# One DMA moved ahead of four others, and the softmax sums of an attention block joined in another order

## The chip, the cores and the metric

The kernel runs on one core of one Trainium2 chip. The metric is the device time of one execution in microseconds (us), as the median of several runs; lower is better.

## The reference

The program computes two transformer layers on one sequence of 2048 tokens with 128 features. The change concerns the first part, the attention of layer 0, and the code just behind it. Cut to what matters:

```python
q = concat([q_c, q_r]);  k = concat([k_c, k_r])        # 8 heads, 128 + 32 features
scores = einsum('bhsd,bhtd->bhst', q, k) * scale       # 2048 x 2048 for each head
attn = softmax(scores, axis=-1)
o = einsum('bhst,bhtd->bhsd', attn, v_c)
x = x + o.reshape(b, s, N_HEADS * D_K) @ W_O + b_O     # then FFN, anchor attention, FFN
```

## The kernel before, in words

The attention works in `NBLK` = 32 blocks: 8 heads times 4 groups of 512 queries. In a block n, the scores stand transposed: 16 tiles of 128 keys by 512 queries. TensorE (PE) makes each with `scores(n, t)` (L1385), ScalarE (ACT) takes the exponential into the ring `prob` (L577), and PE multiplies by the values in two halves of 8 tiles, `weighted(n, 0)` and `weighted(n, 1)` (L1429).

The maximum over the keys must be known before the exponential. So PE also makes the scores in the other orientation (`half_rows`, L1371), and VectorE (DVE) reduces each half row to its maximum (`chunk_max`, L971). These run `LEAD` = 10 slots ahead of the block that uses them. When the maxima of block n+1 are complete, DVE writes `nmx` (`minus_max`, L979), and the sync engine (SP) issues one DMA that copies the 512 values into one row of `q_cols`, the shift row (L463). The first `scores` of block n+1 waits for that DMA. An 8-slot loop on PE and on DVE (`for slot in range(CPB)`) fixes which work stands where: a slot has two score tiles and two half rows. The multiplications by the values stand in slots 1 and 6; `output` (L1413) in slot 3, `totals` (L1440) in slot 4. DVE does `minus_max` in slot 5.

The denominators are the sums of `prob` over the keys. The 16 tiles are first added in 4 groups of 4 tiles (`part`), then `totals` sums each over its partitions. GpSimd (POOL) does these additions in `sums` (L853, L858); for the groups in `VSUM` DVE does the first of three (`begin_sum`, L986), in slots 5 and 6. ACT copies the totals to `den_sb` (L563), SP issues four DMAs (L451, `denominators`) that spread them over partitions, DVE inverts them (L1004, L1006) and adds the scaled output to `X` (`accumulate`, L1020).

SP does its DMAs strictly in program order. In iteration n its loop has the four DMAs of `denominators(n - 2)` first and the shift row of block n after them. In the last block, n = 31, the sums don't go through POOL at all: PE multiplies the 16 `prob` tiles by ones (`last_totals`, L1450), four at a time. Between the blocks PE also takes the transposes of the next layernorm (`ln0_pe`, L337).

PE's results lie in eight banks of PSUM. Half rows, keys, outputs and totals take turns in four of them, so each waits until the item four before it in the turn has been read (`bank_read`).

Of the kernel before, what the change touches and what calls it, by code (L numbers as in the profile page):

```python
# [5 lines left out]
ALU = mybir.AluOpType  # L6
# [6 lines left out]
P = 128  # L13
# [5 lines left out]
def build_kernel(nc, d, out):  # L19
# [13 lines left out]
    with ctx:  # L33
# [157 lines left out]
        VSUM = (2, 3)  # L191
# [7 lines left out]
        part = sb("part", [P, 2, NG, BLK])  # L199
        den_sb = sb("den_sb", [P, BLK])  # L200
# [199 lines left out]
        with nc.Block() as block:  # L400
            @block.sync
            def _(sp):
# [50 lines left out]
                for n in range(NBLK):  # L453
                    k = n % NB
                    if n >= 2:
                        denominators(n - 2)
                    sp.wait_ge(s_sel, n + 1)
                    if n < NB:
                        sp.wait_ge(s_qcol, k + 1)
                    else:  # L460
                        sp.wait_ge(s_sc, NT * (n - NB + 1))
                    with nc.allow_non_contiguous_dma("128 x 4 words into one row"):
                        sp.dma_start(q_cols[SH:SH + 1, k, :].bitcast(F32).rearrange("a (p i) -> a p i", i=TPB),  # L463
                                     nmx[:, n % 2, :].bitcast(F32)).then_inc(s_shift, 16)

# [17 lines left out]
            def _(act):  # L483
# [84 lines left out]
                def exponential(n, t):  # L568
                    g = NT * n + t
                    act.wait_ge(s_sc, g + 1)  # L570
                    if g >= RING and t == 0:
                        act.wait_ge(s_pv, NW * (n - 1) + 1)
                        act.wait_ge(s_sum, ADDS * (n - 1) + 6)
# [30 lines left out]
                for n in range(NBLK):  # L604
                    for t in range(NT):
# [11 lines left out]
                        if n == NBLK - 1 and t == 8:  # L617
                            ln0_act(act, 0, 3)
# [138 lines left out]
            def _(pool):  # L757
# [84 lines left out]
                def sums(n, g):  # L842

                    total = part[:, n % 2, g, :]
                    p = [prob[:, (NT * n + t) % RING, :] for t in range(NG * g, NG * (g + 1))]
                    done = ADDS * n + 3 * g - sum(x < g for x in VSUM)
                    if n >= 2 and g == 0:
                        pool.wait_ge(s_ones, n - 1)
                    if g in VSUM:
                        pool.wait_ge(s_sumd, len(VSUM) * n + VSUM.index(g) + 1)  # L850
                    else:
                        pool.wait_ge(s_exp, NT * n + NG * g + 2)
                        pool.tensor_tensor(total, p[0], p[1], ALU.add).then_inc(s_sum, 1)  # L853
                        done += 1
                        pool.wait_ge(s_sum, done)
                    for x in (2, 3):
                        pool.wait_ge(s_exp, NT * n + NG * g + x + 1)
                        pool.tensor_tensor(total, total, p[x], ALU.add).then_inc(s_sum, 1)  # L858
                        done += 1
                        pool.wait_ge(s_sum, done)  # L860

                for n in range(NBLK - 1):
                    for g in range(NG):
                        sums(n, g)
                        if g == 0 and n < 2:
                            columns(n + 2)
                        if n == NBLK - 2 and g >= 2:
                            ln0_pool(pool, g - 2)
# [52 lines left out]
            def _(dve):  # L921
# [141 lines left out]
                for n in range(NBLK):  # L1063
                    for slot in range(CPB):
# [239 lines left out]
            def _(pe):  # L1304
# [138 lines left out]
                def last_totals(g):  # L1443

                    n = NBLK - 1
                    if g == 0:
                        bank_read(("sums", n))
                    pe.wait_ge(s_exp, NT * n + NG * (g + 1))
                    for x in range(NG):
                        last = pe.matmul(ps[C * x:C * (x + 1), BANK["sums", n], :], ones_v[:, :], prob[:, (NT * n + NG * g + x) % RING, :],  # L1450
                                         start=(g == 0), stop=(g == NG - 1))
                    if g == NG - 1:
                        last.then_inc(s_ones, 1)

# [81 lines left out]
                for n in range(NBLK):  # L1536
                    for slot in range(CPB):
# [33 lines left out]
                        if n == NBLK - 1:  # L1571
                            if slot == 2:
                                last_totals(0)
                                bank_read(("norm", 0))
                                ln0_pe(pe, 0, 3)
                            elif slot == 3:
                                totals(n - 1)
                            elif slot == 4:
                                last_totals(1)
                            elif slot == 7:  # L1580
# [4 lines left out]
                                weigh(n, range(2 * NG, 3 * NG))  # L1585
                last_totals(3)
# [5 lines left out]
                pe.wait_ge(ld_l0, 16 * N_LD_L0)  # L1592
                pe.transpose(ps[0:A, 0, 0:A], anchor[:, :], ident[0:A, 0:A])
                pe.transpose(ps[:, 0, AT_GATE:AT_GATE + E], gate0[:, :], ident[0:E, 0:E]).then_inc(s_an_ps, 1)
                last_denominators()
                output(NBLK - 1)
# [331 lines left out]
```

## Time and profile before

| what | value |
|---|---|
| median of 3 runs | 770.61 us (770.42 to 771.03) |
| the profiled execution's own time | 775.4 us |
| its span in the trace | 773.7 us |
| PE busy (matmuls) | 737.8 us, 95% |
| DVE busy | 626.3 us, 81% |
| POOL busy | 577.4 us, 75% |
| ACT busy | 473.2 us, 61% |
| blocks 2 to 31 of the attention | about 67 to 516 us of the span |

PE's matmuls are pipelined, and the busy time counts overlapping ones, so 95% does not say that PE never waits. A row of a timeline gives the start, the duration, the engine and line, and in brackets how long the engine had been idle before and what ended that. Times of a DMA row on SPq are those of its issue; the landing is told apart.

### The profile page before, as it was taken

How to read it: one execution, taken by the hardware profiler on the slowest of the kernel's cores; microseconds unless marked ns; L12 is line 12 of the kernel's file. 1: busy time of each engine (PE TensorE's matmuls, PEld its weight loads, DVE VectorE, ACT ScalarE, POOL GpSimd, SP SyncE). 2: the span in 40 equal slices, each digit the busy share in tenths (PEclk: the TensorE clock that was granted, in tenths of full speed). 3: DMA queues.
4: the chain of work that ended last, by engine and by line, in shares of the span. 5: the costliest groups of instructions: out<-in, count | busy, mean ns of one | idle time of the engine just before them, and what ended most of it. 6: DMA issues, size and time to landing. Idle time of an engine off the chain costs nothing.

```text
span 773.7 us, 12688 instructions
## 1 busy us (share of the span) xinstructions
PE 737.8 (95%) x4214; PEld 468.8 (61%) x4214; DVE 626.3 (81%) x1305; ACT 473.2 (61%) x1067; POOL 577.4 (75%) x478
## 2 busy tenths in 40 slices
PE   7999999999999999999999999999799999999997
PEld 6655555545545555555554555456556689778885
DVE  7889899998999898999999999933887736876564
ACT  4377666767767666776776766663677841454443
POOL 6489889988989989898998898911689861445554
PEclk9999999999999999999999999997999999999999
DMA  7200000000000000000000000003000000000000
GB/s 155 73 2 1 2 2 2 2 3 1 1 3 1 1 2 2 1 2 2 2 2 3 1 1 2 1 22 93 1 1 0 2 1 2 0 1 16 0 14 27
DMA packets 36616, 8.71 MB, mean 11 GB/s; under 512 B 26580, under 2 KB 35813, under 8 KB 36552
## 3 DMA queue, kind: packets, MB, share of 16 engines
q1 hardware_dynamic: 35272, 7.80, 5.0%
q8 instruction: 33, 0.54, 0.3%
q10 hardware_dynamic: 1280, 0.12, 0.1%
q14 instruction: 31, 0.25, 0.1%
HBM read 6.53 MB, written 1.05 MB: 10 GB/s over the span
## 4 chain that ended last, share of the span: by engine, by line
PE 51%; POOL 12%; issue 10%; DMA 9%; SPq 9%; DVE 5%; ACT 3%; POOLq 0%; DVEq 0%
PE ps L1385 11%; PE ps L1371 10%; SPq L451 9%; DMA q_cols<-nmx 8%; PE ps L1429 8%; POOL hid_lo L917 7%; PE ps L1440 4%; PE ps L1775 4%; PE ps L1413 4%; ACT den_sb L563 2%; POOL nrm L899 2%; POOL hid L899 1%; PE ps L1358 1%; PE ps L1359 1%; DVE mx L971 1%
## 5 line engine op out<-in xcount | busy, mean ns | idle before, releaser
L858 POOL TENSOR_TENSOR part<-part,prob 128x512 f32<-128x512 f32 x248 | 329.3, 1328 | 44.7 <-DVE part L986 17.2
L971 DVE TENSOR_REDUCE mx<-ps 128x1 f32<-128x512 f32 x492 | 310.4, 681 | 36.3 <-PE ps L1371 32.5
L577 ACT ACTIVATE prob<-ps 128x512 f32<-128x512 f32 x512 | 271.1, 604 | 95.6 <-PE ps L1385 95.6
L1385 PE MATMUL ps<-q_cols,key 128*128 128x512 f32 x512 | 217.1, 427 | 13.1 <-DMA q_cols<-nmx 10.8
L1371 PE MATMUL ps<-key,q_rows 128*128 128x512 f32 x512 | 201.3, 397 | 0.8 <-DVE key L957 0.4
L1385 PEld LDWEIGHTS ps<-q_cols,key 128*128 128x128 f32 x512 | 95.5, 188 | 123.0 <-issue 49.9
L1429 PE MATMUL ps<-prob,val 128*32 128x512 f32 x1024 | 123.3, 598 | 0.0
L1371 PEld LDWEIGHTS ps<-key,q_rows 128*128 128x128 f32 x512 | 95.9, 188 | 19.2 <-DVE mx L965 1.4
L917 POOL TENSOR_TENSOR hid_lo<-hid,hid_hi 128x512 fp32r<-128x512 f32 x44 | 56.8, 1295 | 49.6 <-ACT hid_hi L734 49.6
L853 POOL TENSOR_TENSOR part<-prob 128x512 f32<-128x512 f32 x62 | 79.7, 1285 | 4.8
L1429 PEld LDWEIGHTS ps<-prob,val 128*32 128x32 f32 x1024 | 26.7, 109 | 60.9 <-issue 59.6
L718 ACT ACTIVATE act_g<-ps 128x512 f32<-128x512 f32 x44 | 26.4, 599 | 50.8 <-PE ps L1815 50.8
L986 DVE TENSOR_TENSOR part<-prob 128x512 f32<-128x512 f32 x62 | 55.6, 898 | 0.3 <-ACT prob L577 0.3
L1275 DVE TENSOR_TENSOR prod<-ps,act_g 128x512 f32<-128x512 f32 x44 | 30.3, 690 | 31.2 <-PE ps L1815 27.5
L691 ACT ACTIVATE pT<-ps 128x128 f32<-128x128 f32 x128 | 33.7, 279 | 10.6 <-PE ps L1752 10.6
L555 ACT COPY u_sb<-ps 128x512 f32<-128x512 f32 x32 | 18.8, 588 | 34.1 <-PE ps L1429 34.1
L1020 DVE SCALAR_TENSOR_TENSOR X<-ps,rden,X 128x128 f32<-128x128 f32 x128 | 35.7, 341 | 1.3 <-PE ps L1413 1.2
L1813 PE MATMUL ps<-hT_hi,w_hi 128*128 128x512 f32 x88 | 35.4, 403 | 0.0
L1413 PEld LDWEIGHTS ps<-proj,u_sb 128*128 128x128 f32 x256 | 33.4, 191 | 2.6
L1814 PE MATMUL ps<-hT_hi,w_lo 128*128 128x512 f32 x88 | 34.7, 394 | 0.0
L1815 PE MATMUL ps<-hT_lo,w_hi 128*128 128x512 f32 x88 | 34.6, 394 | 0.0
L1413 PE MATMUL ps<-proj,u_sb 128*128 128x128 f32 x256 | 33.8, 275 | 0.0
(278 smaller groups left out, 1085.8 us busy)
## 6 DMA issues: line engine op xcount, KB each, us to landing
den<-den_sb SPq DMA_DIRECT2D x124, 2.0 KB, 2.1
X<-in_L_attn_h_t_dram SPq DMA_DIRECT2D x4, 256.0 KB, 4.4
out_dram<-X SPq DMA_DIRECT2D x4, 256.0 KB, 2.3
w_raw<-in_L_ffn_w_g_dram SPq DMA_DIRECT2D x1, 704.0 KB, 4.4
w_raw<-in_L_ffn_w_u_dram SPq DMA_DIRECT2D x1, 704.0 KB, 7.6
w_raw<-in_L_ffn_w_d_dram SPq DMA_DIRECT2D x1, 704.0 KB, 9.0
w_o<-in_L_attn_W_O_dram SPq DMA_DIRECT2D x1, 512.0 KB
w_out<-in_L_attn_W_out_dram SPq DMA_DIRECT2D x1, 512.0 KB, 5.0
```

What stands on the lines that cost most here:

```text
L451: sp.dma_start(den[:, n % 2, g, :], den_sb[C * g:C * g + 1, :].rearrange("a (p i) -> a p i", i=TPB)).then_inc(s_dend, 16)
L577: act.activation(prob[:, g % RING, :], ps[:, g % 3, :], ACT.Exp, scale=SCALE).then_inc(s_exp, 1)
L853: pool.tensor_tensor(total, p[0], p[1], ALU.add).then_inc(s_sum, 1)
L858: pool.tensor_tensor(total, total, p[x], ALU.add).then_inc(s_sum, 1)
L917: pool.tensor_tensor(hid_lo[:, n % 4, :], hid[:, n % 2, :], hid_hi[:, n % 4, :].bitcast(F32), ALU.subtract).then_inc(s_hlo, 1)
L971: dve.tensor_reduce(mx[:, n % 2, c % TPB, at:at + 1], ps[:, BANK["rows", 2 * lin + j], :], AX.X, ALU.max).then_inc(s_mrd, 1)
L986: dve.tensor_tensor(part[:, n % 2, g, :], prob[:, t % RING, :], prob[:, (t + 1) % RING, :], ALU.add).then_inc(s_sumd, 1)
L1020: last = dve.scalar_tensor_tensor(out=xt, in0=ps[:, BANK["out", n], i * P:(i + 1) * P], scalar=rden[:, n % 2, i:i + 1], in1=xt, op0=ALU.mu ...
L1371: pe.matmul(ps[:, BANK["rows", 2 * lin + j], :], q_rows[:, k, i * P:(i + 1) * P], key[:, h % KBUF, c0:c0 + BLK], start=True, stop=True).th ...
L1385: pe.matmul(ps[:, g % 3, :], key[:, n // NB % KBUF, t * P:(t + 1) * P], q_cols[:, n % NB, :], start=True, stop=True).then_inc(s_sc, 1)
L1413: last = pe.matmul(ps[:, BANK["out", n], i * P:(i + 1) * P], u_sb[:, n % 2, i * P:(i + 1) * P], proj[:, n // NB, :], start=True, stop=True)
L1429: last = pe.matmul(ps[C * x:C * (x + 1), U, :], val[:, t, :], prob[:, (NT * n + t) % RING, :], start=(t < NG), stop=(t >= NT - NG))
```

## The change

Four things change. SP issues the shift row of block n ahead of the four DMAs of `denominators(n - 2)`. `VSUM` becomes (1, 2, 3): DVE also begins the sum of group 1, in slot 2 of every block, and POOL has 9 additions instead of 10. POOL's order changes: tiles 2 and 3 are added to each other into a new tile `pair`, then joined to the sum of tiles 0 and 1. In the last block, POOL and DVE make the sums of groups 0 and 1 as well, PE reads these with two matmuls (`first_totals`) in place of eight, and a few instructions of PE and ACT there stand in another place.

```diff
-        VSUM = (2, 3)
+        VSUM = (1, 2, 3)
...
                 for n in range(NBLK):
                     k = n % NB
-                    if n >= 2:
-                        denominators(n - 2)
                     sp.wait_ge(s_sel, n + 1)
...
                                      nmx[:, n % 2, :].bitcast(F32)).then_inc(s_shift, 16)
+                    if n >= 2:
+                        denominators(n - 2)
...
-                        if n == NBLK - 1 and t == 8:
+                        if n == NBLK - 1 and t == 10:
                             ln0_act(act, 0, 3)
...
+                def first_sums(n):
+                    total = [part[:, n % 2, g, :] for g in range(2)]
...
+                    ready(n, 1)
+                    add(total[0], tile(0), tile(1))
+                    ready(n, 3)
+                    add(pair[:, n % 2, :], tile(2), tile(3))
+                    if n < 2:
+                        columns(n + 2)
+                    pool.wait_ge(s_sumd, len(VSUM) * n + 1)
+                    ready(n, 6)
+                    add(total[1], total[1], tile(6))
+                    summed(n, 2)
+                    add(total[0], total[0], pair[:, n % 2, :])
+                    ready(n, 7)
+                    summed(n, 3)
+                    add(total[1], total[1], tile(7))
...
                 for n in range(NBLK - 1):
...
+                    first_sums(n)
+                    last_sums(n)
+                    if n == NBLK - 2:
+                        ln0_pool(pool, 0)
+                        ln0_pool(pool, 1)
+                first_sums(NBLK - 1)
...
+                        if slot == 2:
+                            begin_sum(n, VSUM[0])
...
                         if slot == 5 and n < NBLK - 1:
                             minus_max(n + 1)
-                            begin_sum(n, VSUM[0])
+                            begin_sum(n, VSUM[1])
                         if slot == 6 and n < NBLK - 1:
-                            begin_sum(n, VSUM[1])
+                            begin_sum(n, VSUM[2])
...
+                def first_totals():
+
+                    n = NBLK - 1
+                    pe.wait_ge(s_sum, ADDS * n + 5)
+                    for g in range(2):
+                        pe.matmul(ps[C * g:C * (g + 1), BANK["sums", n], :], ones_v[:, :], part[:, n % 2, g, :], start=False, stop=False)
...
                         if n == NBLK - 1:
-                            if slot == 2:
-                                last_totals(0)
+                            if slot == 3:
+                                totals(n - 1)
+                            elif slot == 4:
                                 bank_read(("norm", 0))
                                 ln0_pe(pe, 0, 3)
-                            elif slot == 3:
-                                totals(n - 1)
-                            elif slot == 4:
-                                last_totals(1)
```

The order of SP's DMAs around blocks 4 to 6, before (a name `den<-den_sb` with x4 is one `denominators`, `q_cols<-nmx` is one shift row):

```order
L463 DMA q_cols<-nmx 1x128x4
L451 DMA den<-den_sb 128x1x4 x4
L463 DMA q_cols<-nmx 1x128x4
L451 DMA den<-den_sb 128x1x4 x4
L463 DMA q_cols<-nmx 1x128x4
```

and where the loop begins, after the change:

```order
L462 DMA q_cols<-nmx 1x128x4 x3
L452 DMA den<-den_sb 128x1x4 x4
L462 DMA q_cols<-nmx 1x128x4
L452 DMA den<-den_sb 128x1x4 x4
L462 DMA q_cols<-nmx 1x128x4
```

The shift row of block 2 and of each block behind it now stands in front of the four DMAs that it stood behind.

One block on DVE, from the key correction of slot 1 to that of the next block, before (`mx` is a maximum, `part` a begun sum, `X` the accumulation):

```order
L957 SCALAR_TENSOR_TENSOR key<-ps,kcol,key 128x512
L1004 TENSOR_REDUCE dsum<-den 128x4
L1006 RECIPROCAL rden<-dsum 128x4
L971 TENSOR_REDUCE mx<-ps 128x1 x4
L1020 SCALAR_TENSOR_TENSOR X<-ps,rden,X 128x128 x4
L971 TENSOR_REDUCE mx<-ps 128x1 x4
L979 TENSOR_REDUCE nmx<-mx 128x4
L986 TENSOR_TENSOR part<-prob 128x512
L971 TENSOR_REDUCE mx<-ps 128x1 x2
L986 TENSOR_TENSOR part<-prob 128x512
L971 TENSOR_REDUCE mx<-ps 128x1 x6
```

and after:

```order
L990 SCALAR_TENSOR_TENSOR key<-ps,kcol,key 128x512
L1037 TENSOR_REDUCE dsum<-den 128x4
L1039 RECIPROCAL rden<-dsum 128x4
L1004 TENSOR_REDUCE mx<-ps 128x1 x2
L1019 TENSOR_TENSOR part<-prob 128x512
L1004 TENSOR_REDUCE mx<-ps 128x1 x2
L1053 SCALAR_TENSOR_TENSOR X<-ps,rden,X 128x128 x4
L1004 TENSOR_REDUCE mx<-ps 128x1 x4
L1012 TENSOR_REDUCE nmx<-mx 128x4
L1019 TENSOR_TENSOR part<-prob 128x512
L1004 TENSOR_REDUCE mx<-ps 128x1 x2
L1019 TENSOR_TENSOR part<-prob 128x512
```

The new `part` stands between the maxima of slots 2 and 3, ahead of the `nmx` for which the shift row waits.

The last block on PE, before, from its slot 2 to the end of the attention (`ones_v` marks the sums, `hn` the layernorm, `val` the multiplication by the values):

```order
L1385 MATMUL ps<-q_cols,key 128x512 x2
L1450 MATMUL ps<-prob,ones_v 32x512 x4
L337 MATMUL ps<-ident,hn 128x128 x4
L1385 MATMUL ps<-q_cols,key 128x512 x2
L1440 MATMUL ps<-part,ones_v 32x512 x4
L1385 MATMUL ps<-q_cols,key 128x512 x2
L1450 MATMUL ps<-prob,ones_v 32x512 x4
L1385 MATMUL ps<-q_cols,key 128x512 x4
L1429 MATMUL ps<-prob,val 32x512 x8
```

and after:

```order
L1420 MATMUL ps<-q_cols,key 128x512 x4
L1475 MATMUL ps<-part,ones_v 32x512 x4
L1420 MATMUL ps<-q_cols,key 128x512 x2
L338 MATMUL ps<-ident,hn 128x128 x4
L1420 MATMUL ps<-q_cols,key 128x512 x4
L1464 MATMUL ps<-prob,val 32x512 x8
```

Two groups of four matmuls with ones are gone here (two matmuls come back in slot 7), and the layernorm transposes stand two slots later.

## Rows read from the trace of the kernel before

**Rows 1.** The page's part 4: share of the span by line, in the chain.

```profile
PE ps L1385 11%; PE ps L1371 10%; SPq L451 9%; DMA q_cols<-nmx 8%; PE ps L1429 8%; POOL hid_lo L917 7%; PE ps L1440 4%; PE ps L1775 4%; PE ps L1413 4%; ACT den_sb L563 2%; POOL nrm L899 2%; POOL hid L899 1%; PE ps L1358 1%; PE ps L1359 1%; DVE mx L971 1%
```

**Rows 2.** The chain in order of time: start us, us, what.

```profile
81.52 3.23 DMA q_cols<-nmx
...
289.39 1.94 DMA q_cols<-nmx
...
303.16 0.60 SPq L451
...
303.86 3.38 DMA q_cols<-nmx
```

**Rows 3.** SP's timeline: start us, us to issue, line, DMA.

```profile
66.91 0.55 SPq L463 DMA_DIRECT2D q_cols<-nmx  x1
...
123.90 2.87 SPq L451 DMA_DIRECT2D den<-den_sb  x4
...
301.36 2.40 SPq L451 DMA_DIRECT2D den<-den_sb  x4
...
494.22 0.55 SPq L463 DMA_DIRECT2D q_cols<-nmx  x1
```

**Rows 4.** DVE's timeline in one block.

```profile
295.40 0.17 DVE L1004 TENSOR_REDUCE dsum<-den 128x4 f32<-128x16 f32 x1
...
296.52 2.48 DVE L971 TENSOR_REDUCE mx<-ps 128x1 f32<-128x512 f32 x4 [0.73 <-PE ps L1371]
...
301.38 1.29 DVE L971 TENSOR_REDUCE mx<-ps 128x1 f32<-128x512 f32 x2 [0.15 <-PE ps L1371]
302.70 0.17 DVE L979 TENSOR_REDUCE nmx<-mx 128x4 fp32r<-128x16 f32 x1
302.79 0.90 DVE L986 TENSOR_TENSOR part<-prob 128x512 f32<-128x512 f32 x1
...
304.81 0.83 DVE L986 TENSOR_TENSOR part<-prob 128x512 f32<-128x512 f32 x1
305.56 0.68 DVE L971 TENSOR_REDUCE mx<-ps 128x1 f32<-128x512 f32 x1
```

**Rows 5.** PE's timeline in the same block.

```profile
290.05 0.50 PE L1385 MATMUL ps<-q_cols,key 128*128 128x512 f32 x1
...
290.85 0.40 PE L1371 MATMUL ps<-key,q_rows 128*128 128x512 f32 x1
291.38 0.50 PE L1385 MATMUL ps<-q_cols,key 128*128 128x512 f32 x1
...
296.09 0.39 PE L1371 MATMUL ps<-key,q_rows 128*128 128x512 f32 x1
...
304.51 0.50 PE L1385 MATMUL ps<-q_cols,key 128*128 128x512 f32 x1
```

**Rows 6.** All of L986, and one pair on POOL and DVE that overlaps.

```profile
L986 DVE TENSOR_TENSOR part<-prob x62: 679/839/1787, 49.8 to 494.9; 128x512 f32<-128x512 f32 x62
...
78.70 2.66 POOL L858 TENSOR_TENSOR part<-part,prob 128x512 f32<-128x512 f32 x2
...
80.46 1.45 DVE L986 TENSOR_TENSOR part<-prob 128x512 f32<-128x512 f32 x1
```

**Rows 7.** DMA activity in 40 slices: first 303.6 to 307.4 us, then 289.3 to 291.3 us.

```profile
DMA  0011110001911002300000000110000000000000
...
q8 instruction: 1, 0.02, 2.4%
...
DMA  1011111110000101111111000054300000000000
```

**Rows 8.** PE's timeline in the last block.

```profile
502.85 0.63 PE L337 MATMUL ps<-ident,hn 128*128 128x128 f32 x4 [1.44 <-DVE hn L331]
...
505.53 1.06 PE L1450 MATMUL ps<-prob,ones_v 128*32 128x512 f32 x8
```

**Rows 9.** PE's timeline in block 0, at its slot 5.

```profile
48.58 1.96 PE L1346 MATMUL ps<-w_o,uvT 128*32 128x128 f32 x64 [0.79 <-DVE mx L971]
```

More of the change, by code:

```diff
@@ L199, in build_kernel @@
         part = sb("part", [P, 2, NG, BLK])
+        pair = sb("pair", [P, 2, BLK])
         den_sb = sb("den_sb", [P, BLK])
@@ L572, in exponential @@
                         act.wait_ge(s_pv, NW * (n - 1) + 1)
-                        act.wait_ge(s_sum, ADDS * (n - 1) + 6)
+                        act.wait_ge(s_sum, ADDS * (n - 1) + 5)
                     elif g >= RING and t == NT // 2:
@@ L840, in _ @@
                 add_bias(3)
[L842 to L847, printed above, removed]
-                        pool.wait_ge(s_ones, n - 1)
[L849 to L860, printed above, removed]
@@ L862, in _, with ready, summed @@
-                for n in range(NBLK - 1):
[L863 to L868, printed above, removed]
+                def ready(n, tile):
+                    pool.wait_ge(s_exp, NT * n + tile + 1)
+                def summed(n, count):
+                    pool.wait_ge(s_sum, ADDS * n + count)
@@ new lines, in add, with tile @@
+                def add(out, a, b):
+                    pool.tensor_tensor(out, a, b, ALU.add).then_inc(s_sum, 1)
+                def first_sums(n):
+                    def tile(t):
+                        return prob[:, (NT * n + t) % RING, :]
+                    total = [part[:, n % 2, g, :] for g in range(2)]
+                    if n >= 2:
+                        pool.wait_ge(s_ones, n - 1)
+                    ready(n, 1)
[12 more added lines that the diff above has]
+                    add(total[1], total[1], tile(7))
@@ new lines, in last_sums, with tile @@
+                def last_sums(n):
+                    def tile(t):
+                        return prob[:, (NT * n + t) % RING, :]
+                    total = [part[:, n % 2, g, :] for g in range(NG)]
+                    pool.wait_ge(s_sumd, len(VSUM) * n + 2)
+                    ready(n, 10)
+                    add(total[2], total[2], tile(10))
+                    ready(n, 11)
+                    summed(n, 6)
+                    add(total[2], total[2], tile(11))
+                    pool.wait_ge(s_sumd, len(VSUM) * n + 3)
+                    ready(n, 14)
+                    add(total[3], total[3], tile(14))
+                    ready(n, 15)
+                    summed(n, 8)
+                    add(total[3], total[3], tile(15))
@@ L1445, in last_totals @@
                     n = NBLK - 1
-                    if g == 0:
+                    if g == 2:
                         bank_read(("sums", n))
@@ L1450, in last_totals @@
                         last = pe.matmul(ps[C * x:C * (x + 1), BANK["sums", n], :], ones_v[:, :], prob[:, (NT * n + NG * g + x) % RING, :],
-                                         start=(g == 0), stop=(g == NG - 1))
+                                         start=(g == 2), stop=(g == NG - 1))
                     if g == NG - 1:
                         last.then_inc(s_ones, 1)
+                def first_totals():
[3 more added lines that the diff above has]
+                        pe.matmul(ps[C * g:C * (g + 1), BANK["sums", n], :], ones_v[:, :], part[:, n % 2, g, :], start=False, stop=False)
                 def last_denominators():
@@ L1585, in _ @@
                                 weigh(n, range(2 * NG, 3 * NG))
+                                first_totals()
                 last_totals(3)
@@ L1592, in _ @@
                 pe.wait_ge(ld_l0, 16 * N_LD_L0)
+                last_denominators()
+                output(NBLK - 1)
                 pe.transpose(ps[0:A, 0, 0:A], anchor[:, :], ident[0:A, 0:A])
                 pe.transpose(ps[:, 0, AT_GATE:AT_GATE + E], gate0[:, :], ident[0:E, 0:E]).then_inc(s_an_ps, 1)
-                last_denominators()
-                output(NBLK - 1)
                 for j in range(E // 2):
```

## The prediction

> **What bounds the kernel now.** I read the chain first. By line it gives 9% of the span to the denominators' DMAs on SP (L451) and 8% to the landing of the shift row [rows 1]. Both stand in it once in every block. In order of time the link is the same each time: the fourth den DMA issues (0.60 us), then the shift row, which lands 1.94 us later, and then PE goes on [rows 2]. In the attention PE's program is thus in the chain, but at each block's start it waits for a DMA.
>
> Next, what a block takes. Shift rows go out at 66.91 us and at 494.22 us with 29 blocks between [rows 3]: 427.3 / 29 = 14.73 us each. It is not even. From 289.39 to 303.86 is 14.47 us [rows 2], and I call that a clean block; 17 of the 29 are within 0.1 us of it or below, and four more within 0.5. Eight have a shift row that lands late, 2.3 to 3.4 us after its issue (two of them shown [rows 2]), and a block of up to 15.9 us. 29 x 14.47 = 419.6, so the uneven ones cost 7.7 us in all.
>
> Then the slack in a clean block. On PE the last half row starts at 290.85, and the next score at 291.38 [rows 5]; a pair of such matmuls goes at (290.85 - 290.05) / 3 = 0.23 to 0.27 us apiece, so PE is idle for 0.3 us, and its own work is 14.17 us. On DVE the idle time is 0.73 + 0.15 us [rows 4], so its own work is 14.47 - 0.88 = 13.59 us. DVE is nearly as full as PE. That decides what this change can give.
>
> Why the shift row is late: `nmx` starts at 302.70 [rows 4], but SP is still issuing the four den DMAs, 2.40 us from 301.36 [rows 3], and the shift row leaves at 303.86 [rows 2]. Without them it could leave 0.1 us or so behind `nmx`.
>
> Why some land late: the DMA view of the late one shows a single instruction packet, and activity 9 in the slice near 304.5 us, while the clean one has its burst (5 4 3) at 290.6, 1.2 us behind its issue [rows 7]. PE starts its slot 7 at 304.51 [rows 5]. I take the packet to be PE's own code, fetched at a fixed place in PE's program, and the shift row's words to queue behind it in one DMA engine.
>
> **The change part by part.** All of a clean block's times count from PE's start at 291.38.
>
> 1. *Shift row first.* It takes 302.70 - 291.38 = 11.32 to `nmx`, about 0.2 more to the issue instead of 1.16, then 1.94. PE would be free to start at 13.5, and its own work ends at 14.17. So the gain of this edit alone is PE's idle time, 0.3 us per clean block, and no more.
>
> 2. *One more sum on DVE, ahead of `nmx`.* The price of a `part` on DVE varies. The one at 304.81 held DVE until 305.56, 0.75 us [rows 4]; the median is 0.84 and the shortest 0.68 in duration [rows 6], which is 0.08 us more than what it holds the engine. The one at 80.46 took 1.45 us, and stood beside POOL's pair of additions from 78.70 to 81.36 [rows 6]. So 0.6 if POOL is idle, 1.37 if it is not. I take 0.76, the median, since POOL loses one of ten additions and waits more. DVE's own work becomes 13.59 + 0.76 = 14.35 us, above PE's 14.17. The bounds are 14.2 and 14.96.
>
>    What is queued behind the sum: the maxima of slot 3, `accumulate`, `nmx` and the shift row, 0.76 later. `nmx` comes at 11.32 - 0.15 + 0.76 = 11.93, the shift row lands at 14.1. That is just in time for PE at 14.17. PE's bank waits come close as well.
>
> 3. *Together.* Behind a late block DVE has no backlog, and PE's 14.17 to 14.25 holds; then DVE's 14.35. I take 14.30, a gain of 0.17 in each of the 21 blocks whose shift row is not late: **3.6 us**.
>
> 4. *Late blocks.* The packet goes with PE's slot 7, 13.13 us into the block [rows 5]. The shift row's words need 1.2 to 1.4 us behind the issue at 12.1, so they arrive at 13.3 to 13.5 and still find the packet there. The end of the packet sets the landing, not the issue. Gain **0**.
>
> 5. *Den DMAs off the way.* In three blocks the four issues took longer, 2.87 instead of 2.40 in the worst [rows 3]. Some **1.0 us** in all leaves the path. They now go out behind the shift row, until 12.1 + 0.55 + 2.5 = 15.2, and land about 2 us later, by 17.2, or by 18.6 with the 1.4 us that a late shift row lost [rows 2]. DVE wants them in slot 1, now at 295.40 [rows 4] and so 4.0 us into a block, not before 14.3 + 4.0 = 18.3. Covered, but without much room.
>
> 6. *POOL.* One addition fewer, 9 x 1.33 [rows 6] = 12 of 14.3 us. It has idle time, nothing waits for it before PE's slot 4 or ACT's first tile of the next block. 0.
>
> 7. *The last block.* PE loses two groups with ones of 1.06 us [rows 8] (1.0 each as they overlap) and gets half a group back: -1.5. The wait of 1.44 us for `hn` [rows 8] shrinks as the transposes stand later, but ACT's exponentials then set the pace, and DVE waits for the den DMAs of block 29 that go out later. Two small transposes leave the way at the end. **-1.8 us** in all.
>
> 8. *The first block.* In slot 5 of block 0 PE waits 0.79 us for DVE's maxima [rows 9], so the new sum is on the path there: **+0.7 us**.
>
> The sum: -3.6 - 1.0 - 1.8 + 0.7 = **-5.7 us**. The profiled execution took 775.4 us (its span of 773.7 and 1.7 around it), 4.8 more than the median of 770.61; all terms are differences, so I take them off the median: 764.9 us.
>
> The Trainium skill ("SBUF — State Buffer", Who interferes with whom) speaks against part 2: a VectorE instruction with two SBUF inputs contends with a GpSimd instruction that reads SBUF, and whoever comes first holds the shared port for its whole length. By that rule the sum at 80.46 had to wait until 81.36, as the trace agrees, and the new one would cost as much wherever an addition of POOL is under way; by the rule the sum is rival E below at its worst.
>
> **The rivals.**
>
> *B. The late landings go, too.* If the shift row's words are through before the packet starts, the rest of the uneven cost falls away, 7.7 - 1.0 = 6.7 us more: 758.2. For it: the issue moves 0.35 us earlier against PE's place. Against: it would need 0.3 to 0.5 us more.
>
> *C. DVE takes the place of the DMA.* If the new sum holds DVE for 0.88 us, a clean block stays at 14.47, and only parts 5, 7 and 8 are left: 770.61 - 2.1 = 768.5. For it: the median's 0.76 is only 0.12 us below that, and in the new order POOL adds tiles 2 and 3 just when DVE comes to slot 2.
>
> *D. No change.* The den DMAs come late on DVE in some blocks, or the last block gains nothing, and the rest cancels: 770.6.
>
> *E. Slower.* Most new sums run into a POOL addition and hold DVE for 1.37 us. Then DVE's work is 14.96, and 21 blocks lose 0.49: 770.61 + 10.3 - 2.1 = 778.8. It decides from a cost of 0.98 us per sum, where 21 x 0.10 eats the 2.1 us. Against: only a few of the 62 sums took that long, with a median of 0.84 [rows 6].
>
> **How the numbers follow.** A, the forecast, 0.50; B 0.16; C 0.16; D 0.09; E 0.09. The predicted time is A's, 764.9. A, B and C together hold 0.82, so the range goes from 757.5 to 769.3. A measurement of this kernel can tell about 0.2% from no change, 1.5 us. Faster by more: A, B and C, 0.82; within: D, 0.09; slower: E, 0.09.
>
> **What the profile after would show.** The shift row issues before the den DMAs, within 0.2 us of `nmx`, and PE's wait for it is gone in clean blocks, which take 14.2 to 14.4 us; DVE has no idle time before slot 2. Blocks of 15.7 us and more remain, with an instruction packet at the same place. If they are gone, B holds. If DVE is the chain in each block at 14.47 or more and the new `part` lasts over 1 us, C or E. A DVE wait for den<-den_sb in slot 1 would make part 5 wrong.

## The result, and the profile after

| | before | after |
|---|---|---|
| median of 4 runs | 770.82 us (770.42 to 771.03) | 759.38 us (758.21 to 760.2) |
| span of the profiled execution | 773.7 us | 758.4 us |
| PE, DVE, POOL busy | 95%, 81%, 75% | 97%, 84%, 71% |

The ratio is 0.9851, with a 95% interval of 0.9834 to 0.9868: 11.4 us faster. The forecast was 5.7 us faster, with a range that holds 759.38.

The two profiled spans differ by 15.3 us, 4 more than the medians. Behind the attention, the profiled execution of before had a stretch at a lower granted clock. In the view by windows (window, length, then busy time of PE, PEld, DVE, ACT and POOL, the granted clock of PE, DMA share, GB/s) it is 0.63 there, between PE's two levels of 1.2 and 2.4 GHz:

```profile
530.00:540.00 10.00, 9.97 (x35) 5.53 (x35) 1.74 (x5) 2.39 (x6) 1.60 (x2) 0.63 0.00 0
```

From the first matmul of L1691 to the first of L1708 (L1731 and L1748 after the change) PE takes 9.92 us in that execution (527.62 to 537.54) and 5.41 us in the one of after (515.92 to 521.33). I leave these 4.5 us out of the account.

The chain of after, by engine and by line, answers to [rows 1]:

```profile
PE 63%; POOL 12%; issue 11%; DVE 9%; DMA 3%; ACT 1%; POOLq 0%; DVEq 0%
PE ps L1420 15%; PE ps L1464 14%; PE ps L1406 13%; POOL hid_lo L950 7%; DVE mx L1004 4%; PE ps L1815 4%; PE ps L1475 3%; PE ps L1448 3%; DMA q_cols<-nmx 3%; POOL nrm L932 2%; POOL hid L932 1%; PE ps L1393 1%; PE ps L1394 1%; DVE X L1053 1%;
```

SP's issues have left it (9% before), and the landing of the shift row has gone from 8% to 3%. SP's timeline (start, us to issue) answers to [rows 3]:

```profile
66.59 0.47 SPq L462 DMA_DIRECT2D q_cols<-nmx  x1
...
298.28 0.52 SPq L462 DMA_DIRECT2D q_cols<-nmx  x1
298.89 3.14 SPq L452 DMA_DIRECT2D den<-den_sb  x4
...
484.58 0.52 SPq L462 DMA_DIRECT2D q_cols<-nmx  x1
```

The 29 blocks take 484.58 - 66.59 = 418.0 us, 14.41 each (14.73 before). A clean one is now 14.20 us (14.47 before). Six are late (eight before), 15.03 to 15.55 us long; what they have over 14.20 adds up to 5.9 us (7.7 before). So of 9.3 us in the blocks some 7.5 come from the clean length and 1.8 from the late ones.

DVE's timeline in a clean block, which answers to [rows 4]:

```profile
334.98 1.29 DVE L1004 TENSOR_REDUCE mx<-ps 128x1 f32<-128x512 f32 x2 [0.40 <-PE ps L1406]
336.18 0.71 DVE L1019 TENSOR_TENSOR part<-prob 128x512 f32<-128x512 f32 x1
336.81 1.28 DVE L1004 TENSOR_REDUCE mx<-ps 128x1 f32<-128x512 f32 x2
...
341.55 0.17 DVE L1012 TENSOR_REDUCE nmx<-mx 128x4 fp32r<-128x16 f32 x1
341.64 0.69 DVE L1019 TENSOR_TENSOR part<-prob 128x512 f32<-128x512 f32 x1
```

and POOL's in the same block:

```profile
335.05 1.29 POOL L851 TENSOR_TENSOR pair<-prob 128x512 f32<-128x512 f32 x1
336.97 1.29 POOL L851 TENSOR_TENSOR part<-part,prob 128x512 f32<-128x512 f32 x1 [0.62 <-ACT prob L578]
...
342.40 1.27 POOL L851 TENSOR_TENSOR part<-part,prob 128x512 f32<-128x512 f32 x1 [1.65 <-DVE part L1019]
```

Set the two side by side. The new sum (336.18) falls almost wholly into POOL's 0.62 us of idle time, the one behind `nmx` (341.64) into the 1.65 us, and they last 0.7 us. All of them together, with min, median and max in ns, against [rows 6]:

```profile
L1019 DVE TENSOR_TENSOR part<-prob x94: 680/701/1356, 45.7 to 493.4; 128x512 f32<-128x512 f32 x94
```

The median fell from 839 to 701 ns. The new sum holds DVE for 336.81 - 336.18 = 0.63 us.

A late block, in PE's timeline:

```profile
299.65 0.50 PE L1420 MATMUL ps<-q_cols,key 128*128 128x512 f32 x1
...
301.47 0.50 PE L1420 MATMUL ps<-q_cols,key 128*128 128x512 f32 x1 [0.62 <-DMA q_cols<-nmx]
```

and the DMA activity from 298 to 302 us, 0.1 us to a slice, which answers to [rows 7]:

```profile
DMA  0000000000000083000001121000000000111110
...
q8 instruction: 1, 0.02, 1.5%
```

The shift row issued at 298.28 has its words at 299.4, 1.1 us later, and the instruction packet is there in the same slice (8). The row lands after 3.15 us and PE waits. Of the row's packets, 135 are through by 299.7 us, against 144 at the same place in the next block, which is clean. The missing nine are a sixteenth, the share of one of the 16 DMA engines, and they come later. It is so in all six late blocks. I call the distance from the issue to PE's slot 7 (299.65) the **lead**: 1.37 us here, and 1.38 in the clean blocks (0.65 before, [rows 2, 5]). Clean and late blocks have the same lead; only the packet differs. PE needs the row about 1.0 us behind the start of its slot 7, so at this lead 2.4 us behind the issue.

### The profile page after: what moved, and what is told of

The parts are those of the page before. It is cut to its first block, busy times and chain, and to the rows that moved or that the text cites. A ratio compares the mean times of both kernels' runs of the same rounds, so it can differ in the third digit from the quotient of the medians.

```text
span 758.4 us, 12606 instructions
## 1 busy us (share of the span) xinstructions
PE 732.4 (97%) x4202; PEld 467.2 (62%) x4202; DVE 634.2 (84%) x1337; ACT 470.5 (62%) x1067; POOL 535.2 (71%) x452
## 4 chain that ended last, share of the span: by engine, by line
PE 63%; POOL 12%; issue 11%; DVE 9%; DMA 3%; ACT 1%; POOLq 0%; DVEq 0%
PE ps L1420 15%; PE ps L1464 14%; PE ps L1406 13%; POOL hid_lo L950 7%; DVE mx L1004 4%; PE ps L1815 4%; PE ps L1475 3%; PE ps L1448 3%; DMA q_cols<-nmx 3%; POOL nrm L932 2%; POOL hid L932 1%; PE ps L1393 1%; PE ps L1394 1%; DVE X L1053 1%; PE ps L338 1%
## 5 line engine op out<-in xcount | busy, mean ns | idle before, releaser
L851 POOL TENSOR_TENSOR part<-part,prob 128x512 f32<-128x512 f32 x188 | 248.6, 1328 | 86.7 <-DVE part L1019 56.8
L1420 PE MATMUL ps<-q_cols,key 128*128 128x512 f32 x512 | 214.9, 422 | 5.4 <-DMA q_cols<-nmx 4.8
L1019 DVE TENSOR_TENSOR part<-prob 128x512 f32<-128x512 f32 x94 | 69.3, 738 | 0.0
L851 POOL TENSOR_TENSOR pair<-prob 128x512 f32<-128x512 f32 x32 | 41.4, 1293 | 1.9 <-ACT prob L578 1.8
L851 POOL TENSOR_TENSOR part<-prob 128x512 f32<-128x512 f32 x32 | 41.4, 1295 | 0.0
L851 POOL TENSOR_TENSOR part<-part,pair 128x512 f32<-128x512 f32 x32 | 41.0, 1282 | 0.0
```

The source lines that it names most:

```text
L851: pool.tensor_tensor(out, a, b, ALU.add).then_inc(s_sum, 1)
L1019: dve.tensor_tensor(part[:, n % 2, g, :], prob[:, t % RING, :], prob[:, (t + 1) % RING, :], ALU.add).then_inc(s_sumd, 1)
L1420: pe.matmul(ps[:, g % 3, :], key[:, n // NB % KBUF, t * P:(t + 1) * P], q_cols[:, n % NB, :], start=True, stop=True).then_inc(s_sc, 1)
```

## The experiments

Each was timed against the kernel before on the same chip. On the four chips used that kernel took 770.7, 770.9, 771.0 and 772.4 us, so times of different experiments compare to within 1 or 2 us only. The first four take the change apart.

**1. The shift row alone.** The kernel before with this edit:

```diff
-                    if n >= 2:
-                        denominators(n - 2)
                     sp.wait_ge(s_sel, n + 1)
...
                                      nmx[:, n % 2, :].bitcast(F32)).then_inc(s_shift, 16)
+                    if n >= 2:
+                        denominators(n - 2)
```

> The kernel before, with the one edit that SP issues the shift row ahead of the den DMAs. Theory: PE's own work of 14.17 to 14.2 us sets a clean block, and a late landing needs a packet of PE's code that starts within about 1.3 us behind the issue. Without the third DVE sum the issue falls at about 11.4 us of the block, 1.8 us ahead of the packet at slot 7, so the late landings vanish: 29 x (14.73 - 14.2) = 15 us less, about 755.5 us. Rival 1: late landings come whatever the distance, six to eight of about 1 us remain: about 762 us. Rival 2: POOL, with its ten additions of 1.3 us and DVE's sums beside them, holds the block at 14.4 or more: 765 us or above.

Measured: 766.16 us, ratio 0.9948 (0.9935 to 0.9961). No block is late any more, but every block with keys takes 14.55 to 14.6 us, more than a clean one of before. DVE's and POOL's timelines, DVE first:

```profile
298.73 0.17 DVE L979 TENSOR_REDUCE nmx<-mx 128x4 fp32r<-128x16 f32 x1
298.81 1.46 DVE L986 TENSOR_TENSOR part<-prob 128x512 f32<-128x512 f32 x1
300.20 1.27 DVE L971 TENSOR_REDUCE mx<-ps 128x1 f32<-128x512 f32 x2
```

```profile
297.07 2.66 POOL L858 TENSOR_TENSOR part<-part,prob 128x512 f32<-128x512 f32 x2
300.41 2.97 POOL L858 TENSOR_TENSOR part<-part,prob 128x512 f32<-128x512 f32 x2 [0.68 <-POOL part L858]
```

POOL's additions end at 299.73; the sum of DVE that starts at 298.81 ends 0.54 us after that, at 300.27, and POOL's next addition, which adds to this sum, starts at 300.41. (The row names POOL's own last addition as what ended the wait; that was done 0.68 us before.) The sum has cost 1.4 us instead of 0.6, and in the chain of a block DVE's `part` has 9%. In the kernel before `nmx` and this sum came later against POOL's additions, because PE's whole block waited for the DMA. So the DMA swap took one wait away and laid bare another. At the end of the attention it costs something too: the four DMAs of block 29 go out behind the shift row, DVE waits 1.29 us for them, and PE, which needs DVE's `hn`, waits 2.73 us at 497.07 instead of 1.44 [rows 8].

**2. Everything but the swap.** The changed kernel with the four DMAs ahead of the shift row again.

> The changed kernel with SP's order of before: den DMAs first, the shift row behind them. Theory: the end of the four den DMAs still sets the shift row, a clean block stays at 14.47 us and the late landings stay, so only the last block's edits count, 2 us: about 768.5 us. Rival: the sums' new order gives part of the steady gain by itself (DVE or POOL held the blocks): 765 us or less.

Measured: 769.76 us, ratio 0.9994 (0.9973 to 1.0016). Clean blocks 14.51 us, late ones remain. SP still holds the row:

```profile
301.41 2.40 SPq L452 DMA_DIRECT2D den<-den_sb  x4
303.91 0.55 SPq L464 DMA_DIRECT2D q_cols<-nmx  x1
```

Without the swap the rest gives nothing that can be measured.

**3. The last block alone.** The edits to block 31 and behind it, in the kernel before.

> The kernel before with the edits of the last block alone (POOL makes the sums of groups 0 and 1 of block 31, PE reads them with first_totals, the layernorm transposes stand two slots later, the anchor transposes behind the output). Theory: 2.2 us less, 768.6 us. Rival: POOL's two first additions more, which DVE begins in the changed kernel, delay first_totals, and it gains nothing: 770.8 us.

Measured: 769.41 us, ratio 0.9998 (0.9982 to 1.0014). This doesn't tell it from nothing. In the trace the end of the attention is shorter by 1.7 us (part 7 below).

**4. Swap and last block.** Experiments 1 and 3 together, still with two sums on DVE and POOL's old order.

> The kernel before with the shift row first and the last block's edits, but without the third DVE sum and POOL's new order. Theory: the two gains add up and there are no late landings: about 753.5 us, 6 us below the changed kernel. Rival: the third DVE sum is what relieves POOL and lets blocks run at 14.2 us; without it 760 us or more.

Measured: 763.36 us, ratio 0.9915 (0.9903 to 0.9928), blocks of 14.57 us, none late. Against experiment 1 the last block is worth 2.8 us by the medians. That is outside the interval of experiment 3; by the traces it is 1.3 us here (part 7 below). My theory of the swap fell here as in experiment 1; the rival held, that something in POOL's work makes the 14.2 us possible.

**5. The third sum without the new order.** The kernel of 4 with `VSUM` = (1, 2, 3), POOL adding as before:

```diff
-        VSUM = (2, 3)
+        VSUM = (1, 2, 3)
...
+                        if slot == 2:
+                            begin_sum(n, VSUM[0])
```

> The changed kernel with GpSimd's additions joined in the old order (0+1, +2, +3 for the first four tiles, no pair), so the shift row first, the last block's edits and VectorE's third sum in slot 2 all stay. Theory 1 (the third sum is what brings the block from 14.57 to 14.20 us, because GpSimd has one addition less and is idle when VectorE's sum behind nmx runs): 758 to 761 us, clean blocks 14.2 us, the sum behind nmx 0.7 us. Rival (the new order of GpSimd's additions is what keeps the two apart): 762 to 765 us as with the shift row and the last block alone (763.4), blocks 14.5 us, the sum behind nmx about 1.4 us.

Measured: 773.97 us, ratio 1.0038 (1.0026 to 1.0051): slower than the kernel before, and 10.6 us slower than experiment 4. My theory fell and the rival's 762 to 765 was still too low. Clean blocks take 14.54 us and seven are late again, at 15.87 to 15.89. DVE in slot 2, then POOL:

```profile
345.94 1.02 DVE L989 TENSOR_TENSOR part<-prob 128x512 f32<-128x512 f32 x1
346.88 1.28 DVE L974 TENSOR_REDUCE mx<-ps 128x1 f32<-128x512 f32 x2
```

```profile
345.13 5.71 POOL L858 TENSOR_TENSOR part<-part,prob 128x512 f32<-128x512 f32 x4
```

The new sum holds DVE for 0.94 us instead of 0.63. The clean block is longer than in the changed kernel by 0.34: about the same amount. Against experiment 4, though, a clean block is not longer (14.57 there). What the third sum costs here are the late blocks, 7 x 1.33 = 9.3 us, and the last three, 14.54 us each instead of 13.96, 13.60 and 13.85. The lead fell from 1.60 to 1.38.

**6. More work for DVE.** The changed kernel with one more instruction in slot 2:

```diff
+                    if g == VSUM[0]:
+                        dve.tensor_reduce(twice[:, :], prob[:, t % RING, :], AX.X, ALU.max)
                     dve.tensor_tensor(part[:, n % 2, g, :], prob[:, t % RING, :], prob[:, (t + 1) % RING, :], ALU.add).then_inc(s_sumd, 1)
```

> The changed kernel with one more instruction on VectorE in slot 2 of every block: a maximum over one 128x512 tile whose result nobody reads (some 0.6 us, as one mx reduction of 512 columns). VectorE has 0.40 us of idle time in a clean block of 14.20 us. Theory 1 (VectorE is within half a microsecond of being the bound, and nmx comes 0.6 us later): blocks 14.4 to 14.7 us, TensorE waits for mx or for the shift row in every block, 764 to 772 us. Rival (TensorE bounds the block with room behind it): 759 to 761 us, blocks 14.2 us as before.

Measured: 777.76 us, ratio 1.0089 (1.0068 to 1.0111), above what I had given either way. Clean blocks take 14.77 us, and five are late. The instruction holds DVE for 0.59 us and the block grows by 0.57. I had counted on DVE's 0.40 us of idle time as cover:

```profile
347.63 1.29 DVE L1005 TENSOR_REDUCE mx<-ps 128x1 f32<-128x512 f32 x2 [0.42 <-PE ps L1409]
348.84 0.68 DVE L1021 TENSOR_REDUCE twice<-prob 128x1 f32<-128x512 f32 x1
349.43 0.68 DVE L1022 TENSOR_TENSOR part<-prob 128x512 f32<-128x512 f32 x1
```

The idle time stands ahead of the maxima of slot 2, where DVE waits for PE, and can't be used for what comes behind them. From slot 2 to `nmx` DVE has no idle time, and PE needs the banks that DVE frees there. In this stretch the slack is nil already in the changed kernel.

**7. PE's code moved.** The changed kernel with six more matmuls at PE's start, where it waits anyway (`spin(14, U)` to `spin(20, U)`). Nothing in the loop changes.

> The changed kernel with six more idle-time matmuls (24 TensorE instructions) at TensorE's start, where it waits anyway: the loop is the same, only the place in TensorE's code at which each packet of instructions is fetched moves by 24 instructions, some 2.1 us of a block. Theory 1 (a block is late where the packet of TensorE's code starts just ahead of the landing of the shift row): the late blocks are others than the 6 at 81, 125, 168, 212, 298 and 455 us, each late one again has a packet from about 0.2 us ahead of the end of slot 7 on; 5 to 8 of them, 758 to 761 us. Rival (the late blocks are late for something in the blocks themselves, such as the denominators' transfers): the same 6 blocks are late, 759.4 us.

Measured: 761.07 us, ratio 0.9874 (0.9855 to 0.9894). Again six blocks are late, but they are those whose shift rows go out at 166.2, 252.4, 296.4, 340.1, 383.7 and 427.6 us: two of them are as in the changed kernel, four others, and four that were late are clean. In the one from 296.40 the packet is again where the row's words are (296 to 300 us):

```profile
DMA  0000000000000007410000111111000000000011
```

So the packet of PE's code is the cause, as the prediction had taken it. Not all of the late blocks moved, as I had written they would. This kernel is 1.7 us slower than the changed one. Its late blocks explain 0.8 of it (6.7 us over 14.20 in all, against 5.9); the rest stays open.

**8. The output later in the block.** Trying for an earlier `nmx`: `output(n - 2)` on PE behind slot 5 instead of 3, `accumulate` on DVE in slot 6.

> The changed kernel with the output matmuls of block n-2 moved on TensorE from slot 3 to behind slot 5, and VectorE's accumulate from slot 3 to slot 6: the row maxima of slot 5, and with them nmx and the shift row, come up to 0.8 us earlier in the block, the work is the same. Theory 1 (the clean blocks are bound by TensorE and the late ones only by the landing of the shift row, which then has room): the shift row is issued 1.7 to 2.2 us ahead of the end of slot 7 (1.38 us in the changed kernel), no late blocks, all 14.2 us: 759.4 less 5.9 us, 752 to 755 us. Rival (VectorE, 0.40 us from its own bound, takes over, or GpSimd's adds meet the sums again): blocks 14.3 to 14.5 us and 757 to 763 us.

Measured: 769.4 us, ratio 0.9985 (0.9965 to 1.0006). No block is late, at a lead of 2.49 us, which bears out the first half of the theory. But each takes 14.78 us. In the chain:

```profile
348.62 1.05 DVE X L1053 x4
...
349.72 0.50 PE ps L1406
```

PE now waits in slot 7 until DVE's `accumulate` has freed the bank. The rival held, at a higher price than it gave.

**9. The weighting later in the block.** The second try: `weighted(n - 1, 1)` in slot 2 instead of slot 1.

```diff
-                        if slot == 1 and n >= 1:
+                        if slot == 2 and n >= 1:
                             weighted(n - 1, 1)
...
-                        if t == 4 and n >= 1:
+                        if t == 6 and n >= 1:
                             sums(n - 1)
```

> The changed kernel with the 16 matmuls of weighted(n-1, 1) moved on TensorE from slot 1 to slot 2 (and ScalarE's copy of their sums from tile 4 to tile 6): the row maxima of slot 2 are there 1.85 us earlier, so that VectorE, whose only idle time in a clean block is the 0.40 us ahead of them, runs through and nmx and the shift row come up to 0.4 us earlier ahead of the end of slot 7 (1.38 us in the changed kernel, about 1.6 us in the kernel with the shift row alone, which had no late blocks). Theory 1: issue 1.6 to 1.8 us ahead, no late blocks, all 14.2 us: 752 to 756 us. Rival 1 (VectorE's sum of slot 2, now 0.4 us earlier, meets GpSimd's addition and takes 1.0 us, as it did with the old order of GpSimd's additions): the shift row is not earlier, late blocks stay, 759 to 765 us. Rival 2 (TensorE waits for VectorE to free a bank in slot 2 instead): blocks over 14.3 us, 762 us or more.

Measured: 785.95 us, ratio 1.0181 (1.0167 to 1.0195), blocks of 15.30 us and every fourth of 15.81. Both rivals hold: the sum of slot 2 meets POOL's pair and takes 1.21 us, and in the chain PE waits for DVE's `key` (26.1 us in all):

```profile
382.62 0.67 DVE key L990
...
383.34 0.50 PE ps L1406
```

**10. The new order with two sums.** The changed kernel, but POOL adds tiles 4 and 5 itself:

```diff
-        VSUM = (1, 2, 3)
+        VSUM = (2, 3)
...
-                    pool.wait_ge(s_sumd, len(VSUM) * n + 1)
+                    ready(n, 5)
+                    add(total[1], tile(4), tile(5))
```

> The changed kernel without VectorE's third sum: GpSimd adds tiles 4 and 5 itself, everything else, the new order with the pair too, stays. GpSimd then has 10 additions of about 1.29 us in a block, 12.9 us and more. Theory 1 (both are needed: GpSimd is only idle beside VectorE's sums when it has an addition less and they are in the new order): the sum behind nmx takes 1.4 us again, blocks 14.5 us, 762 to 766 us. Rival (the new order alone keeps the two apart): the sum behind nmx takes 0.7 us and VectorE has 0.6 us less to do, so clean blocks 14.2 us, nmx earlier and no late blocks: 753 to 757 us.

Measured: **748.7 us**, ratio 0.9701 (0.9685 to 0.9717). The rival won, by more than it asked. Blocks take 14.06 us, none is late, and the last three 13.6 to 13.8. DVE, and then POOL, in one block:

```profile
340.98 2.48 DVE L1005 TENSOR_REDUCE mx<-ps 128x1 f32<-128x512 f32 x4 [0.66 <-PE ps L1405]
...
347.16 0.17 DVE L1013 TENSOR_REDUCE nmx<-mx 128x4 fp32r<-128x16 f32 x1
347.25 0.68 DVE L1020 TENSOR_TENSOR part<-prob 128x512 f32<-128x512 f32 x1
```

```profile
339.57 1.28 POOL L851 TENSOR_TENSOR part<-prob 128x512 f32<-128x512 f32 x1
340.80 1.30 POOL L851 TENSOR_TENSOR pair<-prob 128x512 f32<-128x512 f32 x1
...
345.97 1.30 POOL L851 TENSOR_TENSOR part<-part,prob 128x512 f32<-128x512 f32 x1
```

POOL's last addition ends at 347.27 and DVE's sum starts at 347.25: they just miss each other. The same six additions in experiment 4, POOL and then DVE:

```profile
349.81 1.29 POOL L853 TENSOR_TENSOR part<-prob 128x512 f32<-128x512 f32 x1
351.18 2.66 POOL L858 TENSOR_TENSOR part<-part,prob 128x512 f32<-128x512 f32 x2
...
355.26 2.65 POOL L858 TENSOR_TENSOR part<-part,prob 128x512 f32<-128x512 f32 x2
```

```profile
357.03 1.43 DVE L989 TENSOR_TENSOR part<-prob 128x512 f32<-128x512 f32 x1
```

In the old order an addition needs the one ahead of it, and starts 1.37 us behind it (349.81, 351.18). In the new one neighbours are independent and start 1.23 us apart (339.57, 340.80), except one, tile 6 of group 1, which starts 1.42 us behind the addition that it needs (342.06, 343.48). From the first start to the last end it is 7.70 us against 355.26 + 2.65 - 349.81 = 8.10. DVE's sum stands 7.68 and 7.22 us behind the first of them. So it meets 0.02 us of the last addition in one kernel and 0.88 in the other, and runs 0.75 us longer there. Of the 0.86 us between the two, 0.40 are POOL's shorter row of additions. The other 0.46 are where DVE's sum stands: DVE, which has lost no time to the last sum, waits 0.66 us for PE in slot 2 instead of 0.35. By these numbers the old order would still reach 0.42 us into the sum at that place.

**11. The same without the swap.** Experiment 10 with the four DMAs first.

> The kernel of the last run (the new order of GpSimd's additions with two sums on VectorE, 748.7 us) with the four transfers of the denominators ahead of the shift row again. Theory 1 (the transfers' issue, 2.48 us, holds the shift row as in the kernel before, and no order of the additions helps against that): the shift row is issued at most 0.7 us ahead of the end of slot 7 instead of 1.59, TensorE waits for its landing, clean blocks 14.4 to 14.9 us, late ones on top, 758 to 772 us. Rival (with nmx earlier in the block there is time for them): blocks 14.1 us, 748 to 752 us.

Measured: 768.66 us, ratio 0.9972 (0.9954 to 0.9991), clean blocks 14.47 us, late ones up to 15.7. The theory holds: `nmx` starts at 347.28 for 0.17 us, and the row leaves at 348.44:

```profile
345.93 2.40 SPq L452 DMA_DIRECT2D den<-den_sb  x4
348.44 0.55 SPq L464 DMA_DIRECT2D q_cols<-nmx  x1
```

**12. The packet beside a lead of 1.60 us.** Experiment 10 with the six matmuls of experiment 7.

> The kernel with the new order and two sums on VectorE (748.7 us, shift row issued 1.59 us ahead of the end of slot 7, no late block) with the six more matmuls at TensorE's start that moved the late blocks of the changed kernel to other places. Theory 1 (a lead of 1.59 us is room enough beside a packet of TensorE's code wherever it falls): no block over 14.2 us, 748 to 750 us. Rival (that kernel had no late block only because no packet happened to fall there): 2 to 6 blocks late by 0.8 to 1.4 us, 751 to 756 us.

Measured: 750.09 us, ratio 0.9743 (0.9713 to 0.9773), and from the second block on none over 14.12 us. In experiment 10 itself one packet falls at the start of slot 7 too (291 to 294 us, 0.075 us to a slice):

```profile
DMA  0000000000000000044100900011111100111111
```

The row was issued at 291.11; its words (4 4 1) are through by 292.5, and the packet (9) comes at 292.65, 0.06 us ahead of slot 7 at 292.71. With a lead of 1.60 us the words pass first. Some rows still land late, four in experiment 10 and four in 12, after 2.1 to 2.5 us, but at this lead PE needs a row only after 2.6 us. Packets did not fall everywhere in a block, so these two kernels show no late block for the places where they fell, and not for all.

## Why the forecast was right in sign, and half the size

With the swap and the last block in all of them, the other two parts of the change make a square:

| | POOL's old order | new order |
|---|---|---|
| two sums on DVE | 763.36 us (exp. 4) | 748.7 us (exp. 10) |
| three sums on DVE | 773.97 us (exp. 5) | 759.38 us (the change) |

The order is worth 14.6 to 14.7 us, the third sum costs 10.6 to 10.7. From before to after: swap -4.5, last block -2.8, order -14.7, third sum +10.7: that is -11.3 us, and 11.4 were measured. The entries were measured on different chips; by the ratios the order is worth 14.4 to 16.5 us and the third sum costs 9.5 to 11.6, so that the two rows agree within 0.1 us is chance.

That the result lies in the forecast's range is in part luck. 759.38 is 5.5 us from the forecast and 1.2 us from rival B, for whose sake the range reached down to 757.5. But B's condition, that the late landings go, did not come true. Now the steps of the prediction.

*Part 1, swap: 0.3 us per clean block, down to 14.17.* The size is wrong. By itself the swap makes a clean block longer, 14.57 us, for the sum that runs into POOL's additions. What it gains are the late blocks (7.7 us); the clean blocks and the end of the attention (experiment 1) take part of that back, and 4.5 us are left. The floor was too high as well: PE's own work is at most 14.06 us (experiment 10), so the idle time in a clean block of before was at least 0.41, not 0.3, which I had from two matmul spacings.

*Part 2, the third sum: 0.76 us on DVE.* Held DVE for 0.63 us. The two old sums became shorter at the same time, 0.84 to 0.70 in the median. This term was mis-sized, and with it part 3, which took 14.30 us from it. 14.20 was measured: the 0.17 us in 21 blocks (3.6 us) became 0.27 us in nearly all 29, 7.5 us, and that is most of the 5.7 us that the forecast lacks. That work added to DVE lengthens the clean block was right: experiment 6 gives 0.57 us for 0.59, and 5 gives 0.34 for 0.31, though POOL's order differs there too. The reason given was not. The prediction set all of DVE's work (14.35) against PE's and expected no idle time before slot 2. DVE's own work is 14.20 - 0.40 = 13.80 us, less than PE's, and what holds the block is the stretch from slot 2 to `nmx` alone. Against experiment 10 the clean block is 0.14 longer, and with `nmx` 0.2 us later the lead falls from 1.60 to 1.38, which lets six late landings back in, 5.9 us.

What part 3 did not see are the last blocks, which have no keys to make (`key`, 0.7 us of DVE). There the new sum meets POOL's pair and eats what is saved:

```profile
478.54 1.18 DVE L1019 TENSOR_TENSOR part<-prob 128x512 f32<-128x512 f32 x1
```

They stay at 14.20 us, where experiment 10 has 13.6.

*Part 4, late blocks: gain 0.* The cause was right, the packet of PE's code. "The end of the packet sets the landing, not the issue" holds in a late block: 0.7 us more lead shortened the excess only from 7.7 to 5.9 us. Rival B named what it takes, 0.3 to 0.5 us more than a lead of 1.0 (13.13 - 12.1): 1.38 us was not enough, and at 1.60 us (experiments 1, 4, 10 and 12) not one block is late.

*Part 5, the den DMAs off the way: -1.0.* Not separable from the 1.8 us of part 4. They were covered in the loop, and late once, for block 29, where DVE waits for them:

```profile
489.16 0.18 DVE L1037 TENSOR_REDUCE dsum<-den 128x4 f32<-128x16 f32 x1 [2.35 <-DMA den<-den_sb]
```

*Part 6, POOL: 0.* This is the step that failed most. I counted POOL's busy time, found room, and gave the new order no price. The order is the largest part of the change. It works not through anything that waits for POOL, but through when POOL holds what DVE's sum needs.

The Trainium skill ("SBUF — State Buffer", Who interferes with whom) says that a VectorE instruction with two SBUF inputs and a GpSimd one that reads SBUF lock each other out. The traces agree: 1.46, 1.02 and 1.21 us beside an addition, 0.68 beside none. I had cited it, but only against the new sum, not for the two that were there.

*Part 7, the last block: -1.8.* The shift row is a poor mark for this, since it moved against PE's work; so I take starts of PE. From PE's slot 7 in block 30 to the transposes of `w_out` just behind the attention it takes 24.41 us before and 21.98 after:

```profile
494.52 0.73 PE L1385 MATMUL ps<-q_cols,key 128*128 128x512 f32 x2
518.93 1.04 PE L1606 MATMUL ps<-ident,w_out 128*128 128x128 f32 x8
...
485.52 0.73 PE L1420 MATMUL ps<-q_cols,key 128*128 128x512 f32 x2
507.50 1.04 PE L1646 MATMUL ps<-ident,w_out 128*128 128x128 f32 x8
```

That is -2.4. The edits to the last block alone give -1.7 between the same marks (experiment 3, 22.73) and -1.3 (experiment 4 against 1, 24.36 and 25.70); the medians, 1.3 and 2.8 us, scatter about that.

*Part 8, block 0: +0.7.* Right. PE waits 0.79 us in slot 5 of block 0 as before [rows 9], 0.35 us later in time (first row, after). By its slot 7 in block 1 it is 0.7 us late (second row before, third after):

```profile
48.93 1.84 PE L1381 MATMUL ps<-w_o,uvT 128*32 128x128 f32 x60 [0.79 <-DVE mx L1004]
...
67.48 0.50 PE L1385 MATMUL ps<-q_cols,key 128*128 128x512 f32 x1
...
68.20 0.51 PE L1420 MATMUL ps<-q_cols,key 128*128 128x512 f32 x1
```

The first shift row goes out 0.3 us earlier all the same (66.59 for 66.91), as it no longer waits for the den DMAs.

Between the two slots 7 lie 427.04 us before and 417.32 after. The measured terms are thus +0.7, -9.7 for the blocks and -2.4, in all -11.4 us, as between the medians. The forecast had +0.7, -4.6 and -1.8: of the 5.7 us that it lacks, 5.1 are in the blocks. One profiled execution of each kernel stands behind these terms, and behind the attention the two differ by a further 0.6 us the other way.

## What to carry to other kernels

Two engines that lock each other out have to be laid side by side in time: an engine's free share says nothing, and a joined order that only makes neighbours independent can be worth more than an instruction less. Idle time covers new work only if it stands in the same stretch between two waits. And take a bundle of edits apart even where it wins: here one part, the third sum, cost 10.7 of the 22 us that the others gave, and the kernel without it (748.7 us) is the best of all.

## What the runs showed of the hardware

- PE's own instruction packets delay a small DMA. There are 33 in the span, 0.54 MB, one about every 22 us in the attention. At a lead of 1.38 us (the changed kernel, experiments 5 and 7) all 19 late rows have a packet that starts 1.10 to 1.75 us behind the issue, and miss nine of their 144 packets at their usual place. The landing takes 3.1 to 3.8 us instead of 1.9. Most of these packets start within 0.2 us of the row's first words (1.17 us). Three in experiment 5 start 0.4 to 0.6 us behind them and the row is late all the same, while one at 1.51 us in the changed kernel delays nothing; so the recorded start alone does not tell which row is hit, and why stays open. Which blocks are hit moves with six matmuls at the start (experiment 7).
- A dependent addition on GpSimd, 128x512, starts 1.37 to 1.42 us behind the one it needs, an independent one 1.23 us behind.
